# Splitting the experts' first matrix on GpSimd in 32 slices over eight batches instead of 16 slices over two

## The chip, the core and the metric

The kernel runs on one core of a Trainium2 chip. The metric is the device time of one execution in microseconds (us), the median of several runs. The core has five engines that run their own instruction streams and meet in semaphores: TensorE (PE, matrix products; PEld are its weight loads), VectorE (DVE), ScalarE (ACT), GpSimd (POOL) and SyncE (SP, which issues DMAs). SBUF is the on-chip memory; PSUM holds TensorE's results.

## The reference

A transformer block with attention in front and a mixture of experts behind, on an input of 16 batches x 256 rows x 128 columns:

```python
x = x + layernorm(attn(layernorm(x)))          # 16 heads of 64, causal softmax, gamma and beta
x = x + layernorm(ffn(layernorm(x)))           # 8 experts, the 2 likeliest for each row

for e in range(8):                             # inside ffn
    gate_e = sum(where(top_i == e, top_p, 0))
    hidden = gelu(xt @ w1[e])                  # w1[e] is 128 x 512
    out = out + gate_e * (hidden @ w2[e])
```

## The kernel before

All arithmetic is float32. Products that need full precision are made as three products of a high and a low part: a matrix is split once into `hi` (a cast to the format of fast products) and `lo = in - hi`, and `product3` adds hi x hi, hi x lo and lo x hi. This case is about the split of the experts' first matrix `w1`: `w1_in`, 128 partitions x 4096 columns, becomes `w1_hi` and `w1_lo` (the trace shows all these tiles as `w_in`, `w_hi`, `w_lo`).

The attention stage is a loop over 16 batches, unrolled on every engine. A batch has 8 pairs of heads and is done in `STEPS` = 4 steps (u = 0 to 3) of two pairs each. In a step k, with pairs p = 2k and p + 1:

- TensorE projects q and k of the next pairs (L385 to L387), transposes the probabilities of the pairs before (`p_transpose`, L442, L446, L447), multiplies by the output matrix (L434), by v (L423), and ends with the scores of the two next pairs (L406, L409) and their masks (L414). The first pair's masks raise `s_mm`. At u = 3 the projection waits for `xt_split`, the split of the next batch's input.
- VectorE takes the maxima of the pair's scores out of PSUM (L777, L778, in `maxima`), multiplies the pair before by the reciprocal sums (`normalise_pair`: L788 with 512 columns, then the PSUM copy L798, then L792 with 256 columns, which raises `nrm`), then takes the maxima of pair p + 1 and so on. TensorE's second `p_transpose` of the step waits for that `nrm`. Between them are pieces of work for other batches: layer norms, the router's steps from batch 2 on, and at u = 2 the split of the next input (L770 casts `xt_hi`, L772 subtracts `xt_lo`), at u = 1 the sum `att`, at u = 3 the normalisation `z3`.
- ScalarE does the exponentials and copies out of PSUM.
- GpSimd has small pieces, in one queue and in the order of its `batch(b)`: `inverse_root` (an addition L1474 and a power L1477, 2 columns each) for the layer norms "x", "a", "z" and "f"; the multiplication by gamma and the addition of beta (L1511, L1513, 256 columns); the addition that makes `x1` (L1520, 256 columns); four indirect DMAs in each batch from batch 3 on, that send rows to their experts (`send`, L1533); and the split of `w1` (L1562 the cast, L1564 the subtraction).

In `batch(b)` the split stands in three calls in batches 1 and 2: slices 0 to 2 ahead of `tail` (which has the "a" root and gamma and beta), slices 3 to 5 behind it, slices 6 and 7 behind `tail_end` (the "z" root and `x1`). Each slice waits for one projected pair (`qk_mm`). The slices have 256 columns. TensorE waits for all of them (`w1_ok`) in `first_rows`, at the end of batch 15, ahead of the expert stage.

Of the kernel before, what the change touches and what calls it, by code (L numbers as in the profile page):

```python
# [5 lines left out]
ALU = mybir.AluOpType  # L6
ACT = mybir.ActivationFunctionType
F32 = mybir.dt.float32
# [12 lines left out]
def sandwich_kernel(nc, x, wq, wk, wv, wo, gamma, beta, router_w, w1, w2, out):  # L21
    B, S, D = x.shape
    H, _, E = wq.shape
    NE, _, F = w1.shape
    T = S // P
    NP = H // 2
# [32 lines left out]
    with ExitStack() as ctx:  # L59
# [8 lines left out]
        def sem(name):  # L68
            if name not in sems:
                sems[name] = ctx.enter_context(nc.semaphore(name))  # L70
            return sems[name]
# [122 lines left out]
        qk_mm, qk_sb = sem("qk_mm"), sem("qk_sb")  # L194
        s_mm = sem("s_mm")
# [15 lines left out]
        wk_ld = [sem(f"wk_ld{g}") for g in range(2)]  # L211

        w1_in_f, w1_hi_f, w1_lo_f = (w[:].rearrange("p e f -> p (e f)") for w in (w1_in, w1_hi, w1_lo))
        W1_BATCHES = 2
        W1_SLICE = NE * F // (NP * W1_BATCHES)

        block = ctx.enter_context(nc.Block())

# [9 lines left out]
        def logits_out(attending):  # L228
            first = T * D + (T + 1) * NE if attending else T * D
            return A[:, first:first + T * NE]  # L230

        LAG = 2

        def over_batches(body):
            for b in range(B):
# [5 lines left out]
        def there(b, back=0):  # L241

            return not isinstance(b, int) or 0 <= b - back < B

        STEPS = NP // 2

        def v_turn(b, u):

            if u == STEPS - 1:
                return (0, 0, 4 * b + 5) if there(b, -1) else None  # L250
            return ((1, 0, 4 * b + 2), (0, 1, 4 * b + 3), (1, 1, 4 * b + 4))[u]

        def is_last(b):

            return isinstance(b, int) and b == B - 1
# [116 lines left out]
        def _(pe):  # L372
# [83 lines left out]
            def logits(r, dst, fresh):  # L456

                pe.wait_ge(sem("xfT_sb"), r + 1)
                for t in range(T):
                    last = mm(dst[:, t * NE:(t + 1) * NE], xfT[:, t * P:(t + 1) * P], rw_sb[:],  # L460
                              start=(fresh and t == 0), stop=True, skip_group_check=True)
                last.then_inc(sem("logit_mm"), 1)
# [17 lines left out]
            def step(b, u):  # L480


                k = STEPS * b + u
                p = 2 * k
                c = 2 * u
                more = u < STEPS - 1 or there(b, -1)

# [4 lines left out]
                if more:  # L492
                    if k >= 1:
                        pe.wait_ge(v_done, 4 * b + 1 + u)
                    if u == 2 and there(b, -1):
                        pe.wait_ge(sem("xt_st"), b + 2)
                    if u == STEPS - 1:
                        pe.wait_ge(sem("xt_split"), b + 2)
# [44 lines left out]
                if u == 1 and there(b, 2):  # L543
                    logits(b - 2, logits_out(True), False)
                if is_last(b) and u == STEPS - 1:
                    first_rows()
# [27 lines left out]
            def batch(b):  # L574
                for u in range(STEPS):
                    step(b, u)
# [75 lines left out]
            def rows_T(n, k, it, dst):  # L652
                pe.wait_ge(got_ld[k], 16 * (it + 1))
                if not (isinstance(n, int) and n < 2):
                    pe.wait_ge(sem("g_split"), n)
                for t in range(2):
                    last = nc.tensor.transpose(dst[:, t * P:(t + 1) * P], got[:, k, t, 0:D], ident[:])
                last.then_inc(sem("gT_mm"), 1)
# [43 lines left out]

            def first_rows():

                pe.wait_ge(sem("w1_ok"), NP * W1_BATCHES)
                pe.wait_ge(sem("ffn_ld"), 16 * (NE + 1))
                pe.wait_ge(v_done, 4 * B)
                rows_T(0, 0, 0, M[:, 0:ROWS])
                rows_T(1, 1, 0, M[:, ROWS:2 * ROWS])
# [3 lines left out]
            for it in range(EARLY // RING):  # L713
                e = experts(it * RING, RING)
                for k in range(RING):
                    n = it * RING + k
# [739 lines left out]
        def _(pool):  # L1456
            q = nc.gpsimd
# [13 lines left out]
            def inverse_root(kind, tiles, eps, n):  # L1471

                pool.wait_ge(sem(f"mv_{kind}"), n)
                q.tensor_tensor(ve[kind][:, 0:tiles], mv[kind][:, 0:tiles, 1], eps[:, 0:tiles], ALU.add)\  # L1474
                    .then_inc(sem(f"ve_{kind}"), 1)
                pool.wait_ge(sem(f"ve_{kind}"), n)
                q.tensor_tensor(rstd[kind][:, 0:tiles], ve[kind][:, 0:tiles], half[:, 0:tiles], ALU.pow)\  # L1477
                    .then_inc(sem(f"rstd_{kind}"), 1)
# [25 lines left out]
            pad_ids(0)  # L1504

            pool.wait_ge(sem("gb_ld"), 16 * 2 * T)
            def tail(b):
                inverse_root("a", T, att_eps, b + 1)
                if not is_last(b):
                    pool.wait_ge(sem("z1_done"), b + 1)  # L1510
                    q.tensor_tensor(z2[:], z1[:], gamma_t[:], ALU.mult).then_inc(sem("z_g"), 1)  # L1511
                    pool.wait_ge(sem("z_g"), b + 1)
                    q.tensor_tensor(z2[:], z2[:], beta_t[:], ALU.add).then_inc(sem("z2_done"), 1)  # L1513

            def tail_end(b):
                inverse_root("z", T, ln_eps, b + 1)
                if not is_last(b):
                    pool.wait_ge(sem("z3_done"), b + 1)
                    pool.wait_ge(sem("x_res_ld"), 16 * b + 16)
                    q.tensor_tensor(x1[:, at(b, T, T), :], x_res[:], z3[:], ALU.add).then_inc(sem("x1_done"), 1)  # L1520
# [28 lines left out]
                for m in range(first, n):  # L1549
                    store(m, m % RING, up_mm, 2 * m + 6)  # L1550

            def split_w1(b, first):

                if not (isinstance(b, int) and 1 <= b <= W1_BATCHES):
                    return
                if b == 1 and first == 0:
                    pool.wait_ge(sem("w1_ld"), 16)
                for j in range(first, min(first + 3, NP)):
                    n = NP * (b - 1) + j
                    cs = slice(n * W1_SLICE, (n + 1) * W1_SLICE)  # L1560
                    pool.wait_ge(qk_mm, NP * b + j + 2)
                    q.tensor_copy(w1_hi_f[:, cs], w1_in_f[:, cs]).then_inc(sem("w1_h"), 1)  # L1562
                    pool.wait_ge(sem("w1_h"), n + 1)
                    q.tensor_tensor(w1_lo_f[:, cs], w1_in_f[:, cs], w1_hi_f[:, cs].bitcast(F32), ALU.subtract)\  # L1564
                        .then_inc(sem("w1_ok"), 1)

            def batch(b):
                if isinstance(b, int) and b == LAG + 1:
                    pool.wait_ge(sem("spare_st"), 16 * UNUSED)
                    pad_ids(UNUSED)  # L1570
                if isinstance(b, int) and b == 0:
                    inverse_root("x", T, ln_eps, 2)
                if there(b, 2) and there(b, 1):
                    inverse_root("f", T, ln_eps, b - 1)
                if there(b) and there(b, 3):
                    send(b - 3)
                if there(b) and there(b, 1):
                    split_w1(b, 0)
                    tail(b - 1)
                    split_w1(b, 3)  # L1580
                    tail_end(b - 1)
                    split_w1(b, 6)
                if there(b, -2):
                    inverse_root("x", T, ln_eps, b + 3)

            over_batches(batch)

            inverse_root("f", T, ln_eps, B - 1)
# [52 lines left out]
```

## Time and profile before

| | |
|---|---|
| median of 3 runs | 734.25 us (733.94 to 735.72) |
| the profiled execution | 735.79 us, its span 734.0 us |
| PE busy | 687.1 us, 94% of the span |
| DVE busy | 553.2 us, 75% |
| ACT busy | 521.7 us, 71% |
| POOL busy | 273.2 us, 37% |
| granted TensorE clock | 0.984 of full speed, full until the last slices of the span |
| chain that ended last | PE 65%, ACT 14%, DVE 12%, DMA 3%, issue 3%, POOL 2% |
| attention stage | from the first masks at 15 us to about 545 us |

Busy time is an average over all stages. What a change on one engine is worth is read from the timeline of the stage it touches: which instruction waited, for what, and how long. In a timeline row the first number is the start, the second the duration, in us from the span's start. A bracket gives the idle time ahead of the row and what ended it.

### The profile page before, as it was taken

To read this page: it belongs to the slowest core of one execution; us is meant where nothing else is said; L and a number is where in the kernel's file an instruction comes from. 1 tells how busy PE (TensorE), PEld (TensorE's weight loads), DVE (VectorE), ACT (ScalarE), POOL (GpSimd) and SP (SyncE) were. 2 spreads that over 40 slices of the span, in tenths; PEclk is the share of its full clock that TensorE was granted. 3 is DMA by queue.
4 is the path that set the end of the run, shared out by engine and by line. 5 is a ranking of instruction groups with operands and counts; after the bars stand their busy time and mean duration, and the time that the engine had idled before them with its cause. 6 is when DMAs were issued, how large, how long until landed. Compare 5 with 4: busy or idle time off the path is not lost.

```text
span 734.0 us, 17696 instructions
## 1 busy us (share of the span) xinstructions
PE 687.1 (94%) x5954; PEld 593.1 (81%) x5955; DVE 553.2 (75%) x1914; ACT 521.7 (71%) x1687; POOL 273.2 (37%) x388
## 2 busy tenths in 40 slices
PE   4899999999999999999999999999989999999954
PEld 3688878888888888887888888888868999999921
DVE  5667889888797989888887989898886775444216
ACT  4787777888787877888877878788765664555515
POOL 3022634332323232332323231322322877655535
PEclk9999999999999999999999999999999999999978
DMA  7530000000000000000100000000020234322155
GB/s 182 173 87 8 9 8 12 21 21 18 24 8 23 9 24 8 25 15 16 31 8 23 9 23 8 24 15 10 21 56 24 73 104 132 91 74 84 41 184 174
DMA packets 43701, 34.88 MB, mean 48 GB/s; under 512 B 10624, under 2 KB 40320, under 8 KB 43616
## 3 DMA queue, kind: packets, MB, share of 16 engines
q1 hardware_dynamic: 37984, 23.81, 12.1%
q0 software_dynamic: 4544, 9.45, 3.6%
q8 instruction: 47, 0.77, 0.4%
q10 hardware_dynamic: 1088, 0.54, 0.3%
q14 instruction: 38, 0.31, 0.1%
HBM read 20.22 MB, written 13.56 MB: 46 GB/s over the span
## 4 chain that ended last, share of the span: by engine, by line
PE 65%; ACT 14%; DVE 12%; DMA 3%; issue 3%; POOL 2%; DVEq 1%; SPq 0%; POOLq 0%; ACTq 0%
PE M L684 8%; PE SC L406 8%; PE PT1O L423 8%; PE A L434 5%; PE M L385 4%; ACT prob L1274 4%; PE M L387 4%; PE M L386 4%; PE SC L414 4%; PE SC L409 3%; ACT prob L1268 3%; ACT qk L1263 3%; PE PT1O L442 2%; PE SC L385 2%; PE SC L386 2%
## 5 line engine op out<-in xcount | busy, mean ns | idle before, releaser
L1263 ACT ACTIVATE qk<-M 128x512 f32<-128x512 f32 x127 | 75.9, 598 | 90.0 <-PE M L387 90.0
L1274 ACT ACTIVATE prob<-SC,nmax 128x256 f32<-128x256 f32 x256 | 125.7, 491 | 0.0
L423 PE MATMUL PT1O<-pT,v_sb 128*64 128x256 f32 (+1 forms) x1024 | 98.6, 335 | 0.7 <-ACT pT L1279 0.7
L423 PEld LDWEIGHTS PT1O<-pT,v_sb 128*64 128x64 f32 x1024 | 64.1, 138 | 42.8 <-ACT pT L1279 17.2
L1268 ACT ACTIVATE prob<-SC,nmax 128x128 f32<-128x128 f32 x256 | 95.4, 382 | 3.4 <-DVE nmax L778 3.3
L1544 POOL DMA_INDIRECT expert_rows<-v_sb,got x78 | 77.1, 988 | 46.5 <-ACT v_sb L1418 27.7
L788 DVE TENSOR_TENSOR prob<-prob,rden 128x512 f32<-128x512 f32 x128 | 88.8, 694 | 2.4 <-DVE rden L782 0.2
L1533 POOL DMA_INDIRECT sent_rows<-rec,slot x64 | 66.6, 1040 | 57.7 <-DVE slot L1038 39.3
L778 DVE TENSOR_REDUCE nmax<-SC 128x2 f32<-128x512 f32 x128 | 86.9, 679 | 0.0
L385 PE MATMUL M<-xt_hi,wqk_hi 128*128 128x256 f32 x254 | 82.5, 325 | 3.0 <-DVE xt_lo L772 2.2
L406 PE MATMUL SC<-qk 64*128 64x256 f32 x512 | 84.4, 406 | 0.6 <-ACT prob L1274 0.6
L777 DVE TENSOR_REDUCE nmax<-SC 128x2 f32<-128x256 f32 x128 | 53.1, 415 | 38.6 <-PE SC L414 38.3
L1279 ACT ACTIVATE pT<-PT 128x512 f32<-128x512 f32 x128 | 76.6, 598 | 3.3 <-PE PT L447 3.3
L434 PE MATMUL A<-wo_sb,hT 128*128 128x128 f32 x512 | 77.8, 275 | 0.0
L684 PE MATMUL M<-w_sb,hidT 128*128 x624 | 76.2, 275 | 0.9 <-ACT v_sb L1418 0.9
L684 PEld LDWEIGHTS M<-w_sb,hidT 128*128 128x128 f32 x624 | 72.7, 192 | 1.1 <-issue 1.1
L387 PE MATMUL M<-xt_hi,wqk_lo 128*128 128x256 f32 x254 | 72.1, 284 | 0.0
L386 PE MATMUL M<-xt_lo,wqk_hi 128*128 128x256 f32 x254 | 71.6, 282 | 0.0
L434 PEld LDWEIGHTS A<-wo_sb,hT 128*128 128x128 f32 x512 | 67.1, 192 | 0.0
L447 PE MATMUL PT<-ident,prob 128*128 128x128 f32 x256 | 62.8, 273 | 0.0
L446 PE MATMUL PT<-ident,prob 128*128 128x128 f32 x256 | 62.8, 273 | 0.0
L1418 ACT ACTIVATE v_sb<-M,got 128x128 f32<-128x128 f32 x78 | 24.4, 364 | 52.3 <-PE M L684 52.3
(186 smaller groups left out, 1777.8 us busy)
## 6 DMA issues: line engine op xcount, KB each, us to landing
got<-sent_rows SPq DMA_DIRECT2D x39, 132.0 KB, 2.3
w_in<-expert_rows SPq DMA_DIRECT2D x16, 256.0 KB, 3.6
x_in<-L_attn_x SPq DMA_DIRECT2D x16, 128.0 KB, 2.2
w_in<-L_ffn_w SPq DMA_DIRECT2D x1, 2048.0 KB, 11.6
x_res<-L_attn_x SPq DMA_DIRECT2D x16, 128.0 KB, 2.1
w_sb<-L_ffn_w SPq DMA_DIRECT2D x8, 256.0 KB, 4.8
out<-y_out SPq DMA_DIRECT2D x8, 256.0 KB, 2.1
sent_rows<-pad_rec SPq DMA_DIRECT2D x11, 132.0 KB, 4.5
```

The lines of the kernel that those rows point to most:

```text
L385: mm(dst, a_hi, b_hi, start=start, stop=False, skip_group_check=True)
L386: mm(dst, a_hi, b_lo, start=False, stop=False, skip_group_check=True)
L387: return mm(dst, a_lo, b_hi, start=False, stop=True, skip_group_check=True)
L406: mm(SC[par][:, k, LATE_Q], qk[r, par, 0, P:S], qk[r, par, 1, :], start=True, stop=False, skip_group_check=True)
L423: last = mm(PT1O[k * E:(k + 1) * E, cols], v_sb[:, t, h * E:(h + 1) * E], src[:, par, k, :], start=(t == 0), stop=(t == 1), skip_group_che ...
L434: last = mm(A[:, t * D:(t + 1) * D], hT[:, par, t * P:(t + 1) * P], wo_sb[:, c, :], start=(c == 0 and t == 0), stop=(c == NP - 1), skip_gr ...
L684: last = mm(out_bank[:, t * D:(t + 1) * D], hidT[:, s, c, t * P:(t + 1) * P], w2_e[:, c * D:(c + 1) * D], start=(t == 0 and c == 0), stop= ...
L778: v.tensor_reduce(nmax[:, par, 0, :], SC[par][:, :, LATE_Q], AX_X, ALU.max, negate=True).then_inc(mx, 1)
L788: v.tensor_tensor(prob[:, slot, :, 1:3, :], prob[:, slot, :, 1:3, :], rden[:, par, 0, :].unsqueeze(2).unsqueeze(3).broadcast_to([P, 2, 2, ...
L1263: a.activation(qk[:, p % 2], src[:].rearrange("p (i s) -> p i s", i=2), ACT.Copy).then_inc(qk_sb, 1)
L1268: return a.activation(prob[:, slot, k, 0, :], SC[par][:, k, EARLY_Q], ACT.Exp, bias=nmax[:, par, 1, k:k + 1], accum_out=den[:, par, 1, k:k ...
L1274: return a.activation(prob[:, slot, k, 1:3, :].rearrange("p n t -> p (n t)"), SC[par][:, k, LATE_Q], ACT.Exp, bias=nmax[:, par, 0, k:k + 1 ...
```

## The change

The split has 32 slices of 128 columns in place of 16 of 256. They lie in batches 1 to 8, one in each step. `split_w1(b, u)` waits for `s_mm`, so for the scores of the first pair of step u, instead of a projected pair. The calls in GpSimd's queue: slice 0 at the head of the batch, behind the "x" root that ends the batch before; slice 1 behind the "f" root and ahead of `send`; slice 2 inside `tail`, behind the "a" root; slice 3 inside `tail_end`, behind the "z" root. The count for which TensorE waits in `first_rows` goes from 16 to 32.

```diff
-        W1_BATCHES = 2
-        W1_SLICE = NE * F // (NP * W1_BATCHES)
+        W1_BATCHES = 8
+        W1_SLICE = NE * F // (STEPS * W1_BATCHES)
...
-                pe.wait_ge(sem("w1_ok"), NP * W1_BATCHES)
+                pe.wait_ge(sem("w1_ok"), STEPS * W1_BATCHES)
...
-            def tail(b):
+            def tail(b, between=None):
                 inverse_root("a", T, att_eps, b + 1)
+                if between:
+                    between()
...
-            def tail_end(b):
+            def tail_end(b, between=None):
                 inverse_root("z", T, ln_eps, b + 1)
+                if between:
+                    between()
...
-                for j in range(first, min(first + 3, NP)):
-                    n = NP * (b - 1) + j
-                    cs = slice(n * W1_SLICE, (n + 1) * W1_SLICE)
-                    pool.wait_ge(qk_mm, NP * b + j + 2)
+                n = STEPS * (b - 1) + u
...
+                cs = slice(n * W1_SLICE, (n + 1) * W1_SLICE)
+                pool.wait_ge(s_mm, NP * b + 2 * u + 1)
...
+                split_w1(b, 0)
                 if there(b, 2) and there(b, 1):
                     inverse_root("f", T, ln_eps, b - 1)
+                split_w1(b, 1)
                 if there(b) and there(b, 3):
                     send(b - 3)
                 if there(b) and there(b, 1):
-                    split_w1(b, 0)
-                    tail(b - 1)
-                    split_w1(b, 3)
-                    tail_end(b - 1)
-                    split_w1(b, 6)
+                    tail(b - 1, lambda: split_w1(b, 2))
+                    tail_end(b - 1, lambda: split_w1(b, 3))
```

## Rows read from the trace of the kernel before

**Rows 1.** The page, busy time, share of the span and instructions of each engine.

```profile
PE 687.1 (94%) x5954; PEld 593.1 (81%) x5955; DVE 553.2 (75%) x1914; ACT 521.7 (71%) x1687; POOL 273.2 (37%) x388
```

**Rows 2.** Timeline of TensorE: the masks that close a step (start, duration, instruction).

```profile
73.14 0.61 PE L414 MATMUL SC<-mask,ident_bf 128*128 128x256 bf16 x4
81.93 0.61 PE L414 MATMUL SC<-mask,ident_bf 128*128 128x256 bf16 x4
...
106.97 0.61 PE L414 MATMUL SC<-mask,ident_bf 128*128 128x256 bf16 x4
116.24 0.61 PE L414 MATMUL SC<-mask,ident_bf 128*128 128x256 bf16 x4
125.20 0.61 PE L414 MATMUL SC<-mask,ident_bf 128*128 128x256 bf16 x4
...
175.65 0.61 PE L414 MATMUL SC<-mask,ident_bf 128*128 128x256 bf16 x4
183.60 0.61 PE L414 MATMUL SC<-mask,ident_bf 128*128 128x256 bf16 x4
191.66 0.61 PE L414 MATMUL SC<-mask,ident_bf 128*128 128x256 bf16 x4
```

**Rows 3.** Timeline of all engines in batch 2, steps 2 and 3.

```profile
105.18 0.40 POOL L1562 CAST w_hi<-w_in 128x256 fp32r<-128x256 f32 x1
...
105.66 1.05 POOL L1564 TENSOR_TENSOR w_lo<-w_in,w_hi 128x256 fp32r<-128x256 f32 x1
...
106.05 0.94 DVE L792 TENSOR_TENSOR prob<-prob,rden 128x256 f32<-128x256 f32 x1
...
107.43 0.90 DVE L772 TENSOR_TENSOR xt_lo<-xt_st,xt_hi 128x256 fp32r<-128x256 f32 x1
...
108.47 0.36 PE L385 MATMUL M<-xt_hi,wqk_hi 128*128 128x256 f32 x1 [0.89 <-DVE xt_lo L772]
```

**Rows 4.** Groups of GpSimd by shape: busy us, mean ns | idle before.

```profile
L1474 POOL TENSOR_TENSOR ve_a<-mv_a,att_eps 128x2 f32<-128x2 f32 x16 | 3.2, 198 | 45.3 <-DVE mv_a L750 45.3
...
L1467 POOL CAST ident_bf<-ident 128x128 bf16<-128x128 f32 x1 | 0.3, 289 | 0.1
```

**Rows 5.** Timeline of all engines in batch 4, the beginning of step 3.

```profile
176.38 0.39 DVE L777 TENSOR_REDUCE nmax<-SC 128x2 f32<-128x256 f32 x1
...
176.75 0.70 POOL L1477 TENSOR_TENSOR rstd_z<-ve_z,half 128x2 f32<-128x2 f32 x1
...
177.29 0.68 DVE L788 TENSOR_TENSOR prob<-prob,rden 128x512 f32<-128x512 f32 x1
...
178.22 0.41 DVE L792 TENSOR_TENSOR prob<-prob,rden 128x256 f32<-128x256 f32 x1
...
178.69 0.33 PE L442 MATMUL PT1O<-ident,prob 128*128 128x128 f32 x1
```

**Rows 6.** Timelines: batch 1, step 0, and batch 4, step 3.

```profile
49.76 0.91 POOL L1562 CAST w_hi<-w_in 128x256 fp32r<-128x256 f32 x1
...
50.66 0.41 DVE L792 TENSOR_TENSOR prob<-prob,rden 128x256 f32<-128x256 f32 x1
50.75 0.92 POOL L1564 TENSOR_TENSOR w_lo<-w_in,w_hi 128x256 fp32r<-128x256 f32 x1
...
180.49 0.73 POOL L1520 TENSOR_TENSOR x<-x_res,z 128x256 f32<-128x256 f32 x1 [3.04 <-DVE z L755]
...
180.50 0.75 DVE L1011 CAST topf<-topi 128x16 f32<-128x16 uint32 x1
```

**Rows 7.** Timeline of all engines in batch 5, the beginning of step 0.

```profile
184.06 0.70 POOL L1477 TENSOR_TENSOR rstd_x<-ve_x,half 128x2 f32<-128x2 f32 x1
...
184.97 0.68 DVE L788 TENSOR_TENSOR prob<-prob,rden 128x512 f32<-128x512 f32 x1
```

**Rows 8.** Timeline of GpSimd in batch 4: the first send, and the "a" root behind the sends.

```profile
159.44 1.06 POOL L1533 DMA_INDIRECT sent_rows<-rec,slot  x1 [3.33 <-DVE slot L1038]
...
166.64 0.19 POOL L1474 TENSOR_TENSOR ve_a<-mv_a,att_eps 128x2 f32<-128x2 f32 x1 [2.14 <-DVE mv_a L750]
```

More of the change, by code:

```diff
@@ L213, in sandwich_kernel @@
         w1_in_f, w1_hi_f, w1_lo_f = (w[:].rearrange("p e f -> p (e f)") for w in (w1_in, w1_hi, w1_lo))
-        W1_BATCHES = 2
-        W1_SLICE = NE * F // (NP * W1_BATCHES)
+        LAG = 2
+        STEPS = NP // 2
+        W1_BATCHES = 8
+        W1_SLICE = NE * F // (STEPS * W1_BATCHES)
         block = ctx.enter_context(nc.Block())
@@ L230, in logits_out @@
             return A[:, first:first + T * NE]
-        LAG = 2
         def over_batches(body):
@@ L243, in there @@
             return not isinstance(b, int) or 0 <= b - back < B
-        STEPS = NP // 2
         def v_turn(b, u):
@@ L1550, in early_stores, with split_w1 @@
                     store(m, m % RING, up_mm, 2 * m + 6)
-            def split_w1(b, first):
-                if not (isinstance(b, int) and 1 <= b <= W1_BATCHES):
+            def split_w1(b, u):
+                if not 1 <= b <= W1_BATCHES:
                     return
-                if b == 1 and first == 0:
+                n = STEPS * (b - 1) + u
+                if n == 0:
                     pool.wait_ge(sem("w1_ld"), 16)
-                for j in range(first, min(first + 3, NP)):
-                    n = NP * (b - 1) + j
-                    cs = slice(n * W1_SLICE, (n + 1) * W1_SLICE)
-                    pool.wait_ge(qk_mm, NP * b + j + 2)
[L1562 to L1565, printed above, removed]
+                cs = slice(n * W1_SLICE, (n + 1) * W1_SLICE)
+                pool.wait_ge(s_mm, NP * b + 2 * u + 1)
+                q.tensor_copy(w1_hi_f[:, cs], w1_in_f[:, cs]).then_inc(sem("w1_h"), 1)
+                pool.wait_ge(sem("w1_h"), n + 1)
+                q.tensor_tensor(w1_lo_f[:, cs], w1_in_f[:, cs], w1_hi_f[:, cs].bitcast(F32), ALU.subtract)\
+                    .then_inc(sem("w1_ok"), 1)
             def batch(b):
```

## Prediction

> **What bounds the kernel now.** I read the page first. TensorE is busy for 94% of the span [rows 1], and the chain that ended last runs mostly through it, so GpSimd's own time, a third of the span, is worth nothing by itself. What GpSimd can do is to make another engine late. So the second view is the pace of the steps in TensorE's timeline: the mask products (L414) close the scores of every step, and the distance from one group of them to the next is one step. In undisturbed batches step 3 lasts 7.95 us (175.65 to 183.60) and step 0 lasts 8.06 (183.60 to 191.66). Three steps near the slices of the split are longer: step 3 of batch 1 with 8.79, step 3 of batch 2 with 9.27, step 0 of batch 3 with 8.96 [rows 2]. The steps in which the other slices run show no excess.
>
> Third, the timeline of VectorE and GpSimd in batch 2 tells why. A subtraction of the split (1.05 us) has VectorE's multiplication L792 last 0.94 us where it otherwise lasts 0.41, the xt_lo subtraction L772 lasts 0.90, and TensorE then stands idle for 0.89 us until xt_lo is there [rows 3, 5]. It goes both ways: a GpSimd instruction that comes second is the one that is stretched (the 0.91 us cast behind L788, the 0.92 us subtraction behind L792), and VectorE loses nothing then [rows 6]. VectorE's reductions out of PSUM (L777, L778) and its PSUM copy (L798) are not stretched beside the split. The page SBUF — State Buffer of the Trainium skill (Who interferes with whom) has this as an exclusive port pair of the two engines, given to whoever issues first; the rows agree as to who waits.
>
> **Part 1, what goes.** The three-slice blocks behind the beta addition and behind x1 go from batches 1 and 2, with all that they did to steps 3, 3 and 0. The gain by the masks' pace: 8.79 - 7.95 = 0.84, 9.27 - 7.95 = 1.32, 8.96 - 8.06 = 0.90, in sum 3.06 us [rows 2]. I take all of it, since in batch 2 the stretches of VectorE in that stretch (two of about 0.5 us in rows 3 and smaller ones) are as large as the excess. Nothing else is late next: at the undisturbed pace TensorE itself sets the steps, but for step 3, below.
>
> **Part 2, what comes.** 32 casts and 32 subtractions of 128 columns replace 16 and 16 of 256. A GpSimd cast of 128 columns takes 0.29 [rows 4] against 0.40 for 256 [rows 3]; a two-input instruction takes 0.20 for 2 columns [rows 4] and 0.73 for 256 [rows 6], so 0.20 + 0.53/2 = 0.46 for 128. A slice is 0.29 + 0.08 + 0.46 = 0.83 us, all 32 are 27 us, which fit in GpSimd's idle time. What counts is where each of the four of a batch lies against VectorE:
>
> Step 1 and step 2: GpSimd is free when the masks' signal comes, so slice and first reduction begin together. The reductions keep VectorE for 0.91 us (176.38 to 177.29, rows 5) before L788 reads SBUF. The slice needs 0.83. Cost nothing; the cover is 0.08 us, and beyond it GpSimd is the one that waits.
>
> Step 1 has one more wait: the sends of batches 3 to 8 are now behind the slice and its wait for the scores. The first of four sends began at 159.44, shortly after the scores; it will begin later by at most the slice's 0.83 us, and so will the others. Behind them is ve_a, for which GpSimd had 2.14 us to spare [rows 8]. SP's queue isn't passed by anything, and no wait on another engine asks for these rows sooner. Cost nothing.
>
> Step 0: ahead of the slice is rstd_x (184.06 to 184.76), so the slice begins 0.7 us late, and the subtraction at about 185.13, behind the start of L788 at 184.97 [rows 7]. It waits for L788 and then has VectorE's PSUM copy to itself: L792 begins 0.93 after L788 [rows 5], at 185.90. From the 0.92 us subtraction [rows 6], which held the port for 0.55 us at most after L792 let go (0.33 us into its 0.41, so 50.99, to 51.54, the end less the 0.13 us worked out below), half the columns take 0.28. L788 lets go 0.60 us after its start, at 185.57, by the same 0.08 us ahead of its recorded end; 185.57 + 0.28 = 185.85. Free by 0.05 us. Cost nothing, at worst some tenths in all.
>
> Step 3 is the place where the words "begun when the scores are there" don't hold. Ahead of the slice is rstd_z, which ends at 177.45, 0.16 us after L788 has begun [rows 5]. The cast waits behind L788, runs in the copy, and the subtraction comes up just as L792 does. With a cast of 256 columns the same sequence put the subtraction 0.09 us behind L792 (50.75 against 50.66, rows 6); the cast is now 0.11 shorter, so it comes 0.02 us ahead. Who wins at such a distance: in 13 of 13 batches like the one at 180.49, GpSimd's x1 addition, 0.01 to 0.02 us ahead of a small VectorE cast, made that cast last 0.75 us [rows 6]. (One of the 13 stands in the rows; they run from 113.13 to 513.55.) So I take it that GpSimd wins. The price: in rows 3 L792 was released 0.13 us before the subtraction's end (106.05 + 0.53 against 105.66 + 1.05); here that is 178.20 + 0.46 - 0.13 = 178.53, against 178.22, so 0.31 us. TensorE has no slack for it: L442 begins at 178.69, 0.06 after L792's end [rows 5]. Batch 1 has slack, since the router's steps don't run there; batches 2 to 8 pay: 7 x 0.31 = 2.17 us. The bounds are 0 (VectorE wins) and 0.53, the full stretch of a 256-column subtraction [rows 3, 5]. I take 0.31, the one worked out for this width.
>
> The same page and section of the Trainium skill say that the pair is held for the whole instruction; that is rival (c), and the release in rows 3 ahead of the subtraction's end speaks against it.
>
> **Sum.** -3.06 + 2.17 = -0.89 us. On the profiled execution: span 734.0 to 733.1, with the 1.8 us around it 735.79 to 734.9. That execution stands 1.54 us above the median of the runs, 734.25; so the median goes to 733.4.
>
> **The rivals.** (a) VectorE wins the race in step 3. For it: the subtraction's lead is 0.02 us, out of rows that are read to 0.01; nothing in the trace lies between 0.02 ahead and 0.09 behind. Against it: 13 of 13. It gives -3.06, so 731.2. (b) The race goes either way from batch to batch, half of them paid: -3.06 + 1.08 = -1.98, so 732.3. (c) GpSimd keeps VectorE out until the end of its instruction: 178.20 + 0.46 - 178.22 = 0.44, and 7 x 0.44 = 3.08 against 3.06, so 734.3. It speaks against this that L792 came free before the 1.05 us subtraction ended. (d) Slower: in step 3 a late L792 is a late nrm, a late transposition and a late set of exponentials, and one late step costs what such a step costs before, at least the 0.84 of batch 1, whatever the width. Then 7 x 0.84 = 5.9 against 3.06, so 737.1. It decides from 3.06 / 7 = 0.44 us a step on. Against it: in batch 2 the excess of the step was no more than VectorE's stretches. That the change does nothing where the scores come late isn't a rival of its own: it is the order in step 3 that I have costed.
>
> **How the numbers follow.** Forecast 0.45, (a) 0.30, (b) 0.10, (c) 0.07, (d) 0.08. The likeliest is 733.4. The range reaches down past (a) with 0.4 us for a remnant of VectorE's other waits, 730.8, and up past (c) to 734.9; (d) is left out. A measurement can tell 0.3%, 2.2 us, from no change. Faster by more: (a) nearly whole and a half of (b), 0.33; slower by more: (d), 0.08; within: 0.59. Cases with less time hold most of the chance; the forecast's own range is 732.6 to 734.2.
>
> **What would show it.** In the profile after: steps 3 of batches 1 and 2 and step 0 of batch 3 at 7.95, 7.95 and 8.06 (part 1 right); L792 in step 3 of batches 2 to 8 at about 0.72 instead of 0.41 and those steps at 8.26 (race lost), or L792 at 0.41 with a w_lo subtraction stretched to about 0.8 (race won, rival a). L788 at 0.68 in steps 1 and 2 shows these free; a stretched L792 in step 0 would show my 0.05 us wrong. ve_a should still be preceded by idle time in batches 3 to 8. The prediction is wrong if the three long steps stay long, for then the split wasn't their cause.

## The result, and the profile after

In the comparison that stands with the change the kernel before took 734.15 us (733.94 to 735.72) and the changed kernel 729.6 us (729.58 to 730.27), four runs each: ratio 0.9936, interval 0.9917 to 0.9955. The forecast was 733.4 with a range from 730.8; the result lies below it, and below rival (a) with its 731.2 too. Two later comparisons, on other occasions, gave 0.9951 (0.9933 to 0.9969) and 0.9937 (0.9911 to 0.9964).

The profiled execution of the changed kernel took 729.62 us. The page of the changed kernel, its span, its busy times and its chain:

```profile
span 727.8 us, 17728 instructions
...
PE 685.1 (94%) x5954; PEld 592.4 (81%) x5955; DVE 548.2 (75%) x1914; ACT 521.6 (72%) x1687; POOL 284.8 (39%) x420
...
PE 70%; ACT 14%; DVE 9%; issue 2%; DMA 2%; POOL 2%; DVEq 1%; SPq 0%; POOLq 0%; ACTq 0%
```

Beside [rows 1], GpSimd has 32 instructions more and is busy for 11.6 us longer, and VectorE, with the same 1914 instructions, is busy for 5.0 us less: it is stretched less often.

TensorE's timeline of the changed kernel, the mask products that close the scores of a step, in batches 1, 2 and 3 and again in 4 and 5, which answers to [rows 2] (columns: start, us, engine and line, operation, tiles, shape):

```profile
72.36 0.61 PE L414 MATMUL SC<-mask,ident_bf 128*128 128x256 bf16 x4
80.35 0.61 PE L414 MATMUL SC<-mask,ident_bf 128*128 128x256 bf16 x4
...
105.39 0.61 PE L414 MATMUL SC<-mask,ident_bf 128*128 128x256 bf16 x4
113.36 0.61 PE L414 MATMUL SC<-mask,ident_bf 128*128 128x256 bf16 x4
121.41 0.61 PE L414 MATMUL SC<-mask,ident_bf 128*128 128x256 bf16 x4
...
171.83 0.61 PE L414 MATMUL SC<-mask,ident_bf 128*128 128x256 bf16 x4
179.83 0.61 PE L414 MATMUL SC<-mask,ident_bf 128*128 128x256 bf16 x4
187.89 0.61 PE L414 MATMUL SC<-mask,ident_bf 128*128 128x256 bf16 x4
```

The three long steps are gone: step 3 of batch 1 lasts 7.99 us (8.79 before), step 3 of batch 2 7.97 (9.27), step 0 of batch 3 8.05 (8.96). Step 3 of batch 4 lasts 8.00 against 7.95, and step 0 of batch 5 8.06 in both. I read every other step of the attention in the same way. They are equal within 0.05 us. Steps 3 of batches 4 to 8 are longer by 0.03 us on the mean (8.00, 7.99, 8.32, 8.20, 8.00 against 7.95, 8.00, 8.31, 8.16, 7.96), but that is not the price of a slice: steps 3 of batches 9 to 13, where neither kernel has one, differ by up to 0.04 us too, and neighbouring steps are shorter by as much. The 24 steps from step 1 of batch 3 to step 0 of batch 9 take 199.93 us in the changed kernel and 199.89 in the kernel before.

The span can be cut at two places: the first masks of the kernel, and the last masks of the attention.

| span, us | before the first masks | first to last masks | behind the last masks |
|---|---|---|---|
| kernel before, 734.0 | 14.99 | 527.04 | 191.97 |
| changed kernel, 727.8 | 14.17 | 524.20 | 189.43 |
| difference, -6.2 | -0.82 | -2.84 | -2.54 |

The diff explains the middle column: the three steps give -0.80 - 1.30 - 0.91 = -3.01, and the remaining +0.17 is spread over the other steps in hundredths (in the two later pairs of profiles below this remainder is -0.1 and 0.0). The other two columns were in no step of the prediction.

In the middle column the forecast counted on a loss as well, of 0.31 us in each step 3. VectorE and GpSimd of the changed kernel at the beginning of step 3 of batch 4, which answers to [rows 5]:

```profile
173.52 0.68 DVE L788 TENSOR_TENSOR prob<-prob,rden 128x512 f32<-128x512 f32 x1
...
173.65 0.70 POOL L1565 CAST w_hi<-w_in 128x128 fp32r<-128x128 f32 x1
...
174.12 0.41 DVE L798 COPY pT<-PT1O 128x256 f32<-128x256 f32 x1
...
174.43 0.75 POOL L1567 TENSOR_TENSOR w_lo<-w_in,w_hi 128x128 fp32r<-128x128 f32 x1
174.45 0.41 DVE L792 TENSOR_TENSOR prob<-prob,rden 128x256 f32<-128x256 f32 x1
```

The order is the one that was worked out, the lead of GpSimd's subtraction over L792 too (0.02 us). Yet L792 lasts 0.41 us and the subtraction 0.75 instead of 0.46: VectorE had the port. In batch 1 of the same execution it went the other way:

```profile
73.81 0.74 POOL L1565 CAST w_hi<-w_in 128x128 fp32r<-128x128 f32 x1
...
74.64 0.46 POOL L1567 TENSOR_TENSOR w_lo<-w_in,w_hi 128x128 fp32r<-128x128 f32 x1
...
74.66 0.72 DVE L792 TENSOR_TENSOR prob<-prob,rden 128x256 f32<-128x256 f32 x1
...
77.23 0.73 POOL L1524 TENSOR_TENSOR x<-x_res,z 128x256 f32<-128x256 f32 x1 [2.14 <-DVE z L755]
...
77.67 0.84 DVE L788 TENSOR_TENSOR prob<-prob,rden 128x512 f32<-128x512 f32 x1
```

Here L792 lasts 0.72, the 0.41 + 0.31 that the prediction had priced. The lead is 0.02 us again. The last two rows, 3 us later, show what it cost. VectorE itself made up the 0.31 us: it had 0.30 us of idle time left ahead of the pair's next work. But all that it did before came 0.31 us late, its normalisation z too, and with it GpSimd's addition of x1 (L1524). That addition now reaches 0.29 us into the second L788 of the step, which lasts 0.84 us instead of 0.69.

The end of the span is longer before for a reason that lies in the granted clock. (The table of the time before has the clock full until the last slices of the span; in its slices of 18 us the stretch shown here doesn't stand out.) In the windows view (columns: window, us, busy us and instructions of PE, PEld, DVE, ACT and POOL, granted clock, share and GB/s of DMA) the kernel before, behind the attention:

```profile
546.00:554.00 8.00, 7.62 (x41) 5.62 (x42) 6.79 (x19) 5.21 (x17) 0.72 (x1) 0.57 0.58 145
```

and the changed kernel in the same passage, first its slow stretch and then what follows:

```profile
542.20:546.30 4.10, 4.06 (x24) 3.51 (x26) 3.23 (x10) 3.15 (x15) 0.73 (x1) 0.58 0.74 177
546.30:556.00 9.70, 9.01 (x87) 7.98 (x84) 7.04 (x26) 5.75 (x10) 0.90 (x2) 1.00 0.19 51
```

TensorE's timelines have, in both kernels, the same idle gap ahead of it; before, and then after:

```profile
545.90 0.44 PE L442 MATMUL PT1O<-ident,prob 128*128 128x128 f32 x2 [2.16 <-DVE prob L792]
```

```profile
542.24 0.63 PE L442 MATMUL PT1O<-ident,prob 128*128 128x128 f32 x2 [2.16 <-DVE prob L792]
```

Behind the 2.16 us in which TensorE stood idle, the granted clock falls from 1.00 to the half level (1.2 GHz). It stays there for 6.8 us before and for 3.4 us after. The last group of PV products (L423) begins 16.78 us behind the last masks before and 14.79 after: 1.99 of the 2.54 us. Whether the change brings this, and the 0.82 us at the front, is what half of the experiments below are about.

### The profile page after: what moved, and what is told of

It is laid out like the page before. It is cut to its first block, busy times and chain, and to the rows that moved or that the text cites. A ratio compares the mean times of both kernels' runs of the same rounds, so it can differ in the third digit from the quotient of the medians.

```text
span 727.8 us, 17728 instructions
## 1 busy us (share of the span) xinstructions
PE 685.1 (94%) x5954; PEld 592.4 (81%) x5955; DVE 548.2 (75%) x1914; ACT 521.6 (72%) x1687; POOL 284.8 (39%) x420
## 4 chain that ended last, share of the span: by engine, by line
PE 70%; ACT 14%; DVE 9%; issue 2%; DMA 2%; POOL 2%; DVEq 1%; SPq 0%; POOLq 0%; ACTq 0%
PE PT1O L423 8%; PE SC L406 8%; PE M L684 8%; PE A L434 5%; PE M L385 5%; PE M L387 4%; PE M L386 4%; PE SC L414 4%; ACT prob L1274 4%; PE SC L409 3%; ACT prob L1268 3%; PE PT1O L442 3%; ACT qk L1263 3%; PE PT L447 2%; PE PT L446 2%
## 5 line engine op out<-in xcount | busy, mean ns | idle before, releaser
L423 PE MATMUL PT1O<-pT,v_sb 128*64 128x256 f32 (+1 forms) x1024 | 97.5, 333 | 0.7 <-ACT pT L1279 0.7
L423 PEld LDWEIGHTS PT1O<-pT,v_sb 128*64 128x64 f32 x1024 | 63.5, 137 | 42.4 <-ACT pT L1279 17.9
L788 DVE TENSOR_TENSOR prob<-prob,rden 128x512 f32<-128x512 f32 x128 | 88.1, 688 | 2.4 <-DVE rden L782 0.2
```

Of the source, the lines that this page charges most:

```text
L423: last = mm(PT1O[k * E:(k + 1) * E, cols], v_sb[:, t, h * E:(h + 1) * E], src[:, par, k, :], start=(t == 0), stop=(t == 1), skip_group_che ...
L788: v.tensor_tensor(prob[:, slot, :, 1:3, :], prob[:, slot, :, 1:3, :], rden[:, par, 0, :].unsqueeze(2).unsqueeze(3).broadcast_to([P, 2, 2, ...
```

## The experiments

The theory after the first result (R): the split's place in steps 3 and in the step 0 behind it was what cost time; the change takes that away, and of its own four places a batch only step 3 can still cost something, according to who wins the port. Its rivals: the narrower slices do it, whatever their place; and the change brings the shorter half-clock stretch along (K, the stretch belongs to the kernel) rather than that it differs between executions (P).

The first four kernels ran on a chip on which every kernel takes some 20 us more behind the attention (the kernel before 756.87 us, ratios against that). I compare their steps, and not their ends. The expectations name the distance from the first masks to the last. It came out at 526.38, 526.26, 526.77 and 526.81 us in the four, outside the ranges expected for the theories that the steps bear out: on this chip steps 1 from batch 4 on can be longer by 0.14 us and more (last section). Taken by its number, 526.26 would be in the range of theory B of the second kernel (526 or more), but the kernel without any split has 526.38. There is no profile of the kernel before on this chip, so these four totals can only be compared with each other.

**No split at all.** From the kernel before:

```
-                pe.wait_ge(sem("w1_ok"), NP * W1_BATCHES)
+                pe.wait_ge(sem("w1_ld"), 16)
...
-                v.tensor_copy(w1_e[:, s, 0, :], w1_hi_f[:, bass.ds(e, F)])
-                v.tensor_copy(w1_e[:, s, 1, :], w1_lo_f[:, bass.ds(e, F)]).then_inc(sem("w1_e"), 1)
+                v.tensor_copy(w1_e[:, s, 0, :], w1_in_f[:, bass.ds(e, F)])
+                v.tensor_copy(w1_e[:, s, 1, :], w1_in_f[:, bass.ds(e, F)]).then_inc(sem("w1_e"), 1)
...
-                    split_w1(b, 0)
                     tail(b - 1)
-                    split_w1(b, 3)
                     tail_end(b - 1)
-                    split_w1(b, 6)
```

> Leaves out the split of w1: GpSimd does no slice at all, and the expert stage takes the unsplit w1 for the high and the low part. Everything else is the kernel before. The measure is the distance from the first masks to those of the last step in the trace: 527.0 us in the kernel before, 524.2 in the changed one. Theory A (the slices cost time only by holding up VectorE, and the new places are free): 523.9 to 524.1, the time within 0.3 us of the changed kernel apart from the stretch behind the attention. Theory B (the new places cost something in each of 32 steps that the comparison of the two traces hides): below 523.5. If the clock's low stretch behind the attention (7 us before, 4 us after) belongs to the removal of the slices, it is 4 us here too; if it is only where the stretch happens to begin, anything is possible.

Measured: 753.78 us, ratio 0.9968 (0.9951 to 0.9986). The three steps last 7.84, 7.97 and 8.05 us, against 7.99, 7.97 and 8.05 in the changed kernel. So the split was the whole cause of the three long steps. What it still costs in the changed kernel is 0.15 us in batch 1, where VectorE lost the port, and nothing that can be told in the later batches, not 2.17: from step 1 of batch 3 to step 0 of batch 9 three profiles of the kernel before, which has no slices there, take 199.89, 199.89 and 199.93 us, and three of the changed one 199.93, 199.83 and 199.94.

**Slices of the old width, at the heads of batches alone.** From the kernel before; 16 slices of 256 columns, three in a batch, none behind the beta addition or behind x1:

```
-        W1_BATCHES = 2
-        W1_SLICE = NE * F // (NP * W1_BATCHES)
+        W1_BATCHES = 6
+        W1_SLICES = 16
+        W1_SLICE = NE * F // W1_SLICES
...
-                for j in range(first, min(first + 3, NP)):
-                    n = NP * (b - 1) + j
+                for j in range(3):
+                    n = 3 * (b - 1) + j
+                    if n >= W1_SLICES:
+                        break
...
                     split_w1(b, 0)
                     tail(b - 1)
-                    split_w1(b, 3)
                     tail_end(b - 1)
-                    split_w1(b, 6)
```

> The kernel before with its 16 slices of 256 columns, but none behind the beta addition or behind x1: three slices at the head block of each of batches 1 to 5, one in batch 6. Theory A: only the place counted, so the masks' distance falls from 527.0 to 524.0 to 524.3 us, as in the changed kernel, with no slice narrower. Theory B (the width and the one-slice-per-step pacing made the gain): at most 1 us less than before, 526 or more, since VectorE is held as long in all.

TensorE's masks of this kernel, the end of batch 1 and of batch 2 (the line is L415 here):

```profile
72.68 0.61 PE L415 MATMUL SC<-mask,ident_bf 128*128 128x256 bf16 x4
80.51 0.61 PE L415 MATMUL SC<-mask,ident_bf 128*128 128x256 bf16 x4
...
105.54 0.61 PE L415 MATMUL SC<-mask,ident_bf 128*128 128x256 bf16 x4
113.51 0.61 PE L415 MATMUL SC<-mask,ident_bf 128*128 128x256 bf16 x4
121.56 0.61 PE L415 MATMUL SC<-mask,ident_bf 128*128 128x256 bf16 x4
```

Measured: 752.98 us, ratio 0.996 (0.9938 to 0.9983), and steps of 7.83, 7.97 and 8.05 us, as without the split. So slices of the old width with the old wait leave the three steps short as well: the place made them long. This kernel has no race in step 3 either. It isn't free, though. VectorE, batch 4, step 1, where the second and third slice run behind the sends:

```profile
162.59 1.15 DVE L789 TENSOR_TENSOR prob<-prob,rden 128x512 f32<-128x512 f32 x1
```

L789 is the L788 of the other kernels, and lasts 0.68 or 0.69 undisturbed. Steps 1 of batches 4, 5 and 6 last 9.70, 9.70 and 9.62 us, against 9.53, 9.52 and 9.51 without a split, and from step 1 of batch 3 to step 0 of batch 9 this kernel takes 201.15 us against 200.54. So three slices in a row at the heads cost 0.6 us there, while the places of the change, one slice at a time, cost nothing that could be told in these batches on the other chips.

**The change with slices of 256 columns, in four batches.** From the changed kernel:

```
-        W1_BATCHES = 8
+        W1_BATCHES = 4
```

> The changed kernel with slices of 256 columns in batches 1 to 4, at the same places. Theory A: in steps 0 to 2 a slice (1.21 us) outlasts the reductions (0.91 us) and L788 is stretched by 0.1 to 0.2 us, but L442 comes late enough in these steps to hide it; in step 3 the subtraction begins 0.09 us behind L792 and VectorE wins. Masks' distance 524.0 to 524.5. Theory B (each stretch of VectorE reaches TensorE): 12 steps x 0.2 = 2.4 us more, 526.5.

Measured: 753.91 us, ratio 0.9961 (0.9937 to 0.9985). Steps 3 of batches 1 to 4 last 7.84, 8.12, 8.12 and 8.12 us, the last three some 0.15 above those without a split, and steps 0 of batches 3 and 4 8.23 and 8.10 (8.05 without). In step 3 VectorE keeps the port, since the subtraction now comes 0.09 us behind L792, as in [rows 6]. The loss arises in step 2 instead. All engines' timeline of this kernel, batch 2, step 2:

```profile
98.18 0.73 POOL L1567 TENSOR_TENSOR w_lo<-w_in,w_hi 128x256 fp32r<-128x256 f32 x1
...
98.61 0.85 DVE L788 TENSOR_TENSOR prob<-prob,rden 128x512 f32<-128x512 f32 x1
```

L788 lasts 0.85 us instead of 0.68. The slice takes 97.70 to 98.91, 1.21 us, against the 0.91 us of cover by the two reductions. So the cover of the prediction's part 2 is real: 0.83 us fit under it, 1.21 don't, and 0.17 of the excess 0.30 reaches VectorE. Its work in batch 2 follows on almost without idle time, so that L792 of step 3 still begins 0.17 us later than without a split, and TensorE's step 3 is the one that is longer. The longer steps 0 have a stretch of their own: in batch 3 the subtraction lasts 1.05 us and L792 0.62.

**In step 3 the slice in two halves of 64 columns.** From the changed kernel:

```
+                parts = 2 if u == 3 else 1
+                size = W1_SLICE // parts
+                for i in range(parts):
...
+                    cs = slice(n * W1_SLICE + i * size, n * W1_SLICE + (i + 1) * size)
```

> The changed kernel with the slice of step 3 done as two of 64 columns, so that the first subtraction comes about 0.07 us ahead of L792 instead of 0.02. Theory A (the race in step 3 is decided by who comes first, with the line just beyond 0.02 us): GpSimd wins, L792 is held 0.13 to 0.16 us longer in batches 2 to 8, and the masks' distance is 525.1 to 525.4, 1 us above the changed kernel. Theory B (VectorE wins whatever the order there, because the port isn't given back to GpSimd so soon): L792 stays at 0.41 and the distance at 524.2.

All engines' timeline of this kernel, batch 4, step 3:

```profile
173.43 0.68 DVE L788 TENSOR_TENSOR prob<-prob,rden 128x512 f32<-128x512 f32 x1
...
173.56 0.65 POOL L1569 CAST w_hi<-w_in 128x64 fp32r<-128x64 f32 x1
...
174.28 0.33 POOL L1571 TENSOR_TENSOR w_lo<-w_in,w_hi 128x64 fp32r<-128x64 f32 x1
...
174.36 0.53 DVE L792 TENSOR_TENSOR prob<-prob,rden 128x256 f32<-128x256 f32 x1
```

The shorter cast puts the subtraction 0.08 us ahead of L792 instead of 0.02. The lead is 0.07 to 0.08 us in all eight batches. Now GpSimd wins in each of them, L792 lasts 0.53 (0.12 more), and steps 3 last 8.07 or 8.08 from batch 2 to batch 5, 0.10 above the 7.97 of the kernel without a split. Measured: 753.17 us, ratio 0.9954 (0.9938 to 0.9971), which doesn't tell 0.7 us from nothing; the steps do. This is the run that shows the lost race as the prediction had it: once VectorE loses, TensorE's step is late by about as much as L792 (0.10 to 0.15 us against the kernel without a split, for 0.12), from batch 2 on. In batch 1 the step keeps its 7.84 us.

**Both kernels once more.** No edit.

> The kernel before, unchanged, for a trace beside the others of this chip. Steps as in the first trace: three long steps of 8.8, 9.3 and 9.0 us. Theory P (the stretch at half clock behind the attention comes in pieces of 3.4 us, 0, 1 or 2 or 3 of them, by where the idle gap of 2.2 us falls, and the kernel does not choose): its length may differ from the 6.8 us of the first trace. Theory K (it belongs to the kernel): 6.8 us again.

> The changed kernel, unchanged. Attention, first masks to last: 3.0 us (at most 0.2 more or less) under c1. Theory P: the half-clock stretch behind the attention may be 0, 3.4 or 6.8 us; theory K: 3.4 us again. Time: 3.0 us under c1 plus half the difference of their half-clock stretches.

Measured: the kernel before 736.06 us against its other runs of that occasion (734.29), ratio 1.0013 (0.9996 to 1.003); the changed kernel 731.18 (729.44 to 731.78), ratio 0.9951 (0.9933 to 0.9969). The three parts of the span are 15.44, 527.15 and 192.61 us in the one, 14.95, 524.02 and 190.43 in the other. The middle difference is there again (-3.13; this time L792 lost in batch 1 and nowhere else), and so is the half-clock stretch, 6.8 and 3.4 us. At the front the difference is 0.49 instead of 0.82, and at the end 2.18 instead of 2.54. By this run alone, K and P both stand.

**A little more of TensorE work in the attention.** From the changed kernel, to see whether later attention work shifts the half-clock stretch: four extra repeats of one batch's transpositions.

```
-                for t in range(T):
...
+                for _ in range(1 + (4 if b == 12 else 0)):
+                    for t in range(T):
```

> The changed kernel with the transposition of the next input in batch 12 done five times instead of once (eight more transpositions of 128 columns, the same result), about 0.9 to 1.8 us more on TensorE. Nothing else changes, so the end of the attention only comes later. Theory P: the half-clock stretch behind it can change by 3.4 us or a multiple, and the time then by another amount than the work added. Theory K: 3.4 us as in the changed kernel, and the time grows by the work added.

Measured: 730.92 us, ratio 0.9957 (0.9927 to 0.9986). One step lasts 10.23 us instead of 9.35, so 0.88 us were added; the attention is 525.05 us long, the part behind it 189.63, and the half-clock stretch 3.4. A delay of this size in the attention costs what it lasts, and doesn't turn the stretch into the long one. That speaks against the idea that 3 us more of attention would do so by their length, but doesn't exclude it.

**The big memset of the prologue later.** From the changed kernel, and then the same edit from the kernel before:

```
             inverse_root("x", T, ln_eps, 1)
 
+            pool.wait_ge(sem("xn_done"), 1)
             q.memset(ones_bf[:], 1.0)
```

> The changed kernel; GpSimd waits for the first normalised input (xn_done) before it clears the padding records (2112 columns, 1.9 us) and the other constants. In both traces the first normalisation on VectorE lasts 2.2 to 2.8 us instead of 0.6, beside that memset. Theory A (GpSimd's instructions hold VectorE's SBUF-to-SBUF work here too): 0.6 us for it, and the first masks come 1 to 1.6 us earlier (14.2 to 12.6 or 13.2), limited by the weights that come by DMA. Rival (the first masks wait for the weights anyway): no earlier than 0.3 us.

> The kernel before with the memset behind the first normalisation. First masks to last 527.0 to 527.2. The half-clock stretch behind the attention: theory P says 0, 3.4 or 6.8 us, whichever; theory K says 6.8, as in both traces of the kernel before.

The reason for it is in the timeline of all engines, the changed kernel run again, prologue:

```profile
4.91 2.24 DVE L755 TENSOR_SCALAR xn<-x_in,mv_x,rstd_x 128x128 f32<-128x128 f32 x2 [1.12 <-POOL rstd_x L1477]
...
5.14 1.93 POOL L1485 MEMSET pad_rec<- 128x2112 f32 x1
...
14.95 0.61 PE L414 MATMUL SC<-mask,ident_bf 128*128 128x256 bf16 x4
```

and the changed kernel with the memset later:

```profile
4.89 0.60 DVE L755 TENSOR_SCALAR xn<-x_in,mv_x,rstd_x 128x128 f32<-128x128 f32 x2 [1.12 <-POOL rstd_x L1477]
...
14.65 0.71 PE L414 MATMUL SC<-mask,ident_bf 128*128 128x256 bf16 x4
```

The first normalization (L755) falls from 2.24 to 0.60 us, but the first masks come only 0.30 us sooner. Over all runs they come between 13.83 and 15.44 us, and the changed kernel alone had 14.17, 14.95 and 14.51: unchanged kernels differ by more than the memset or the change could be seen to move. What makes them differ, the prologue's loads or something else, no run varied. Measured: 730.3 us, ratio 0.9944 (0.9923 to 0.9966), for the changed kernel with the edit, and 733.76, ratio 0.9977 (0.9949 to 1.0004), for the kernel before with it. Neither is told from its parent. The latter is of use for something else: its attention lasts 527.27 us, as before, and its half-clock stretch is 3.4 us.

**No slice in step 3.** From the changed kernel with the later memset: three slices a batch, in steps 0 to 2, over 11 batches.

```
-                n = STEPS * (b - 1) + u
+                n = 3 * (b - 1) + u
+                if n >= W1_SLICES:
+                    return
...
-                    tail_end(b - 1, lambda: split_w1(b, 3))
+                    tail_end(b - 1)
```

> The changed kernel with the 32 slices in steps 0 to 2 only, over eleven batches (the last with two), and with the memset behind the first normalisation. Theory A (what is left of the split's price lies in step 3): first masks to last 523.7 to 523.9 us, against 524.0 to 524.2 in the changed kernel: 0.15 in batch 1, where L792 is stretched, and 0.02 to 0.03 in each of seven more. Theory B (steps 0 to 2 cost something too): 524.2 or more. The time is not expected to differ from the changed kernel's by more than it can be measured.

Measured: 731.68 us, ratio 0.9944 (0.9921 to 0.9967); first to last masks 524.06 us, against 524.06 in the changed kernel's own run beside it and 524.02 to 524.20 in the others. The three steps last 7.83, 7.94 and 8.05. The expected tenths of a microsecond beyond the changed kernel didn't come out. VectorE won in batch 1 of the run beside it, so that the 0.15 us weren't there to win, and the later batches had nothing to give back: from step 1 of batch 3 to step 0 of batch 9 this kernel takes 199.96 us, against 199.94 with a slice in each step 3. There is nothing more to be had from the split's places.

**Both kernels a third time.** No edit.

> The kernel before, a third trace. Theory P: half-clock stretch of 0, 3.4 or 6.8 us. Theory K: 6.8.

> The changed kernel, a third trace. 3.0 us under c3 between first and last masks. Theory P: half-clock stretch of 0, 3.4 or 6.8 us. Theory K: 3.4.

Measured: the kernel before 735.05 us, ratio 1.0 (0.9975 to 1.0025); the changed kernel 731.36 (729.57 to 733.71), ratio 0.9937 (0.9911 to 0.9964). The windows view of the kernel before, same window as above, and of the changed kernel:

```profile
546.00:554.00 8.00, 8.00 (x62) 6.65 (x62) 7.04 (x20) 6.04 (x18) 0.72 (x1) 0.79 0.57 147
```

```profile
542.40:550.40 8.00, 7.91 (x60) 6.47 (x61) 6.97 (x20) 6.08 (x19) 0.73 (x1) 0.79 0.61 152
```

Both have a mean granted clock of 0.79 over 8 us where the kernel before first had 0.57, and 62 and 60 products of TensorE in the window where it had 41. The stretch is 3.4 us in both. The unchanged kernel can have the short one, so K falls: the stretch was 6.8, 6.8 and 3.4 us in three profiles of the kernel before, 3.4 with the later memset, and 3.4 in all three of the changed one and in the three kernels made from it on these chips. Whether the change makes the short one likelier, so few profiles can't tell. Side by side, with the stretch equal:

| span, us | before the first masks | first to last masks | behind |
|---|---|---|---|
| kernel before, third, 732.2 | 14.84 | 527.23 | 190.13 |
| changed kernel, third, 729.0 | 14.51 | 524.06 | 190.43 |
| difference, -3.2 | -0.33 | -3.17 | +0.30 |

All that is left of the gain is in the attention, where the diff acts.

## Why the prediction was right or wrong

**Part 1, the three long steps: right.** -3.06 was forecast; they gave -3.01 in the changed kernel's profile (-0.80, -1.30, -0.91), and the kernel without a split has them at the same lengths but for 0.15 us in batch 1. Nothing was late next but the x1 addition of that batch.

**Steps 1 and 2 free: right, the cover too, but not what lies beyond it.** L788 lasts 0.68 in them. Changed kernel, VectorE and GpSimd in step 1 of batch 4:

```profile
155.07 0.42 DVE L777 TENSOR_REDUCE nmax<-SC 128x2 f32<-128x256 f32 x1 [0.18 <-PE SC L414]
...
155.11 0.29 POOL L1565 CAST w_hi<-w_in 128x128 fp32r<-128x128 f32 x1 [2.78 <-PE SC L414]
155.47 0.46 POOL L1567 TENSOR_TENSOR w_lo<-w_in,w_hi 128x128 fp32r<-128x128 f32 x1
...
156.01 0.68 DVE L788 TENSOR_TENSOR prob<-prob,rden 128x512 f32<-128x512 f32 x1
...
156.25 1.39 POOL L1537 DMA_INDIRECT sent_rows<-rec,slot  x1 [0.32 <-issue]
...
162.86 0.19 POOL L1474 TENSOR_TENSOR ve_a<-mv_a,att_eps 128x2 f32<-128x2 f32 x1 [1.38 <-DVE mv_a L750]
```

Cast and subtraction last the 0.29 and 0.46 us of the estimate and end at 155.93, 0.08 ahead of L788. Beyond the cover, the prediction said, GpSimd is the one that waits. The 256-column kernel showed the contrary: there the subtraction has the port when L788 comes, and VectorE waits (0.85 us instead of 0.68).

**The sends behind the slice: right.** ve_a waited 2.14 us for VectorE before [rows 8] and waits 1.38 now: the sends' delay of 0.76, under the 0.83 given, came out of idle time.

**Step 0 free by 0.05 us: right.** Changed kernel, batch 5, step 0, which answers to [rows 7]:

```profile
180.29 0.70 POOL L1477 TENSOR_TENSOR rstd_x<-ve_x,half 128x2 f32<-128x2 f32 x1
...
180.96 0.29 POOL L1565 CAST w_hi<-w_in 128x128 fp32r<-128x128 f32 x1
...
181.20 0.68 DVE L788 TENSOR_TENSOR prob<-prob,rden 128x512 f32<-128x512 f32 x1
...
181.33 0.87 POOL L1567 TENSOR_TENSOR w_lo<-w_in,w_hi 128x128 fp32r<-128x128 f32 x1
...
182.13 0.42 DVE L792 TENSOR_TENSOR prob<-prob,rden 128x256 f32<-128x256 f32 x1
```

The subtraction waits behind L788, ends at 182.20, 0.07 behind the start of L792, and L792 lasts 0.42: the release ahead of the recorded end, which the working took from rows 3, was needed and was there.

**Step 3: the step that failed.** The working of place and price was right (lead 0.02 us; 0.31 us where VectorE loses, measured in batch 1; 0.10 to 0.12 for 64 columns), but not the winner. In the five profiles with 128-column slices in step 3 the lead was 0.01 to 0.03 us in each batch; in batches 2 to 8 VectorE kept the port 35 times of 35, and in batch 1 GpSimd took it 4 times of 5. The term +2.17 us of the sum measured nothing that can be told. The fault lies in the precedent: the 13 of 13 in rows 6 were against a small cast of VectorE (L1011), of another kind and with other work ahead of it than L792, and were carried over because their distance was the same. Against L792 itself the trace of before had one case only near this distance, with VectorE first (0.09 us), which says nothing of the order here. So the trace of before couldn't decide the race, and 0.45 against 0.30 claimed more than it held. At 0.07 to 0.08 us of lead GpSimd won 8 of 8 against L792, so the turning point lies between; two recorded starts 0.02 us apart don't tell which request came first. What makes batch 1 differ stays open; the router's steps don't run there, so other work stands ahead of L792, but no run varied that. Not even there does the kernel fix the winner: in the third profile of the changed kernel VectorE has it, with the same lead of 0.02 us.

The bounds were 0 to 0.53 us a step; it was 0, the lower bound, as far as the batches' lengths tell. Of rival (d), a late step costing more than VectorE's lateness, nothing was seen, also where VectorE did lose (0.10 to 0.15 for 0.12 us in the kernel with halves, 0.15 for 0.17 in the one with 256 columns). In batch 1 the slack that the prediction gave that batch did take up all of the 0.31 us (VectorE stands idle there for 0.30 us, against 0.62 in the third profile). The 0.15 us by which the step is longer came by a path that the prediction didn't have: the x1 addition was late with VectorE's z and met L788. In the third profile, where VectorE won, the addition ends before L788 begins, L788 lasts 0.69 and the step 7.83 us. Rival (c), a port held to the end of the instruction, would have made L792 last 0.85 in batch 1; it lasted 0.72. This is the place where the Trainium skill (SBUF — State Buffer, "Who interferes with whom") says that the pair is held for the whole instruction, and the measurement decides: VectorE goes on some 0.13 us before the recorded end (0.13 again with 64 columns). Whether the instruction has then done its last access, and only its record runs on, the trace doesn't tell. What the page says of whoever issues first can't be read from recorded starts this close.

**From the span to the median: wrong in the range.** The sum was made on an execution at 735.79 us and moved by the same 1.54 us to the median. The steps in fact gave -2.84 to -3.17 in three pairs of profiles, which is 0.9957 to 0.9961 of 734.25, and the three comparisons gave 0.9936, 0.9951 and 0.9937. The first interval ends at 0.9955, just short of it; the other two (to 0.9969 and 0.9964) hold it. What part of the 4.55 us between the first medians is chance and what part belongs to the change is not settled: a half-clock stretch of 3.4 instead of 6.8 us is worth some 2 us in a profile, the kernel before had both in different executions, and the executions that were only timed carry no trace that would tell how often. So the second step that failed is the taking over of the steps' sum to the median with 0.4 us to spare below it; the race explains 2.2 us of the 3.8 by which the forecast was off, and the other 1.6 stay open. The range was too narrow there in any case: below rival (a) it had 0.4 us, while single runs of the kernel before went from 732.75 to 737.69 within one comparison.

## What to carry to other kernels

Look in the trace for the neighbour that a filler instruction delays, and move the filler under work that doesn't use the shared port; here the slices in three steps were worth 3 us. Slices of the old width in other places got these 3 us too, and lost 0.6 of them where three ran in a row. When two engines reach for a port within a few hundredths of a microsecond, cost both outcomes, and don't carry over the winner from another pair of instructions, however often it was seen there. When an engine loses a few tenths, follow also what it triggers on the other one: the slack of the first doesn't cover that. Before the difference of two profiled spans is explained, cut it by stages and profile both kernels again: 3.4 of the 6.2 us here lay in stages that the change doesn't touch, and none of it was left when the unchanged kernel had the short half-clock stretch too.

## What the runs showed of the hardware

- The same idle gap of TensorE (2.15 to 2.17 us), in the same kernel, is followed by 6.8 or by 3.4 us at the half clock (granted 0.50, 1.2 GHz). On the other chip, where the gap is 2.31 us, it was followed by 6.8 us without a split, and by none with slices of 256 columns at the batches' heads (granted 1.00 from 545 to 553 us). Between two profiles of the kernel before, the long and the short stretch differ by 1.9 us up to the last group of PV products.
- A memset of GpSimd that only writes (2112 columns, 1.93 us) stretched two VectorE instructions that read and write SBUF (L755) from 0.60 to 2.24 us together in the record.
- On the chip with 20 us more behind the attention, step 1 from batch 4 on lasts 9.51 us without a split, instead of 9.37. VectorE there waits for TensorE's logits, in the kernel without a split:

```profile
194.22 0.42 DVE L1054 TENSOR_TENSOR att<-xn,A 128x256 f32<-128x256 f32 x1 [1.85 <-PE A L460]
```

and in the kernel with the halves, whose sends begin behind a slice:

```profile
192.87 0.42 DVE L1054 TENSOR_TENSOR att<-xn,A 128x256 f32<-128x256 f32 x1 [0.88 <-PE A L460]
```

With the slice ahead of the sends the step lasts 9.38, and in the same kernel 9.54 from batch 9 on, where there are no slices; with 256 columns in four batches it goes to 9.50 from batch 5 on. On the other chips both kernels have 9.37. So on this chip the step is 0.14 us longer where the sends begin at once, and not where a slice stands ahead of them. Whether the sends' start or the slice itself does it, and why only there, stays open.
